# Order of SyncE's transfers in a group, and of two steps of VectorE in the seventh tile

## The reference

```python
q = rope(rms_norm((x @ Wq.T)))                      # 16 heads
k = rope(rms_norm(concat(context, x) @ Wk.T))       # 4 heads, 1857 rows
v = concat(context, x) @ Wv.T
x = x_before + softmax(q @ k.T * SCALE) @ v @ Wo.T
# then: 32 routed experts (6 per token) and a shared one,
# a windowed latent attention over the same context, a small quantised feed-forward
```

## Time and profile before

| | us |
|---|---|
| runs | 1920.83, 1919.81, 1908.78 |
| median | 1919.81 |
| profiled execution | 1917.32 |
| its span, first to last instruction | 1915.5 |
| mean granted clock of TensorE | 0.949 of 2.4 GHz |

### The profile page before, as it was taken

How to read it: one execution, slowest core, us unless ns; L and a number is a source line. 1 busy time by engine, 2 the same in 40 slices (tenths; PEclk the granted TensorE clock), 3 DMA queues, 4 the chain that set the end, 5 groups by cost and what they waited for, 6 DMA issues and landing times. The chain is left out here.

```text
span 1915.5 us, 42600 instructions
## 1 busy us (share of the span) xinstructions
PE 1684.7 (88%) x14901; PEld 1305.6 (68%) x15047; DVE 1422.2 (74%) x3606; ACT 1157.2 (60%) x2910; POOL 1123.2 (59%) x1718
## 2 busy tenths in 40 slices
PE   4899988998999899999898989897899888479987
PEld 3677776787787677777676777675565555339974
DVE  7898886887878788788686868776767565575746
ACT  6577775776777577677665767664325544173533
POOL 5678684786856768568484766741037776182210
PEclk8899999999999999999999999999799999795998
DMA  3210212112020221211113121244639998400100
GB/s 122 73 52 28 68 59 75 52 53 84 24 65 18 76 80 52 68 41 54 53 47 103 52 80 47 68 125 143 219 98 308 304 297 262 179 25 20 45 10 25
DMA packets 117150, 174.91 MB, mean 91 GB/s; under 512 B 13738, under 2 KB 82195, under 8 KB 116691
## 3 DMA queue, kind: packets, MB, share of 16 engines
q1 hardware_dynamic: 106130, 139.99, 22.7%
q0 software_dynamic: 9984, 30.42, 5.2%
q10 hardware_dynamic: 832, 1.84, 0.3%
HBM read 129.04 MB, written 43.16 MB: 90 GB/s over the span
## 5 line engine op out<-in xcount | busy, mean ns | idle before, releaser
L939 DVE TENSOR_TENSOR att_pT<-att_pT 128x512 bf16<-128x512 f32 (+1 forms) x512 | 320.6, 650 | 203.1 <-ACT att_pT L744 200.4
L580 PE MATMUL att_out<-att_V,att_pT 128*128 128x128 bf16 x5760 | 394.9, 221 | 38.3 <-DVE att_pT L939 36.0
L580 PEld LDWEIGHTS att_out<-att_V,att_pT 128*128 128x128 bf16 x5760 | 355.1, 99 | 68.7 <-DVE att_pT L939 53.7
L744 ACT ACTIVATE att_pT<-att_pT 128x512 bf16<-128x512 f32 (+1 forms) x512 | 277.7, 572 | 104.2 <-PE att_pT L566 104.2
L750 ACT ACTIVATE att_prob<-att_scores,att_negmax 128x512 f32<-128x512 f32 (+1 forms) x512 | 329.8, 654 | 17.6 <-DVE att_negmax L928 16.9
L557 PE MATMUL att_scores<-att_K,att_Q 128*128 128x512 bf16 (+1 forms) x1408 | 298.5, 359 | 7.4 <-DVE att_Q L900 0.5
L926 DVE TENSOR_REDUCE att_mx<-att_scores 128x1 f32<-128x512 f32 (+1 forms) x512 | 291.1, 629 | 0.8 <-PE att_scores L557 0.6
L566 PE MATMUL att_pT<-att_ident,att_prob 128*128 128x128 f32 x1920 | 275.7, 275 | 0.0
L557 PEld LDWEIGHTS att_scores<-att_K,att_Q 128*128 128x128 bf16 x1536 | 150.8, 98 | 144.2 <-issue 2.1
L566 PEld LDWEIGHTS att_pT<-att_ident,att_prob 128*128 128x128 f32 x1920 | 210.3, 142 | 1.0
L480 PE MATMUL att_aux<-att_wkv,att_kvT 128*128 128x256 bf16 x1350 | 173.5, 279 | 20.7 <-DVE att_aT L900 16.1
(11 more groups left out here) (352 smaller groups left out, 3302.4 us busy)
## 6 DMA issues: line engine op xcount, KB each, us to landing
moe_wu<-wu_s SPq DMA_DIRECT2D x80, 352.0 KB
att_stage<-in_we_l SPq DMA_DIRECT2D x32, 528.0 KB, 4.7
wu_s<-att_windows SPq DMA_DIRECT2D x32, 352.0 KB, 2.8
moe_wd<-wd_s SPq DMA_DIRECT2D x80, 128.0 KB
att_wq<-wq_s SPq DMA_DIRECT2D x12, 512.0 KB, 4.2
att_wo<-wo_s SPq DMA_DIRECT2D x12, 512.0 KB, 3.8
wd_s<-att_windows SPq DMA_DIRECT2D x32, 176.0 KB, 3.0
att_stage<-in_ctx_l SPq DMA_DIRECT2D x9, 512.0 KB, 4.3
```

The lines of the kernel that those rows point to most:

```text
L580: last = nc.tensor.matmul(out_ps[:, i % 2, :], pT[:, i % 2, a, k, :], V[:, par, k, w, :], start=(k, a, w) == (0, 0, 0), stop=(k, a) == (KT ...
L744: nc.scalar.activation(pT[:, i % 2, 0, 4 * j:4 * j + m, :], pT_ps[j % 2][:, 0:m, :], ACT.Copy).then_inc(s["pt_hi"], 1)
L939: nc.vector.tensor_tensor(pT[:, i % 2, 1, 4 * j:4 * j + m, :], pT_ps[j % 2][:, 0:m, :], pT[:, i % 2, 0, 4 * j:4 * j + m, :], ALU.subtract) ...
```

## The change

In SyncE's program of a group the jobs of this group are listed first (`here`), and those of slot 0 (`early`). Behind L409 come now the stage load for the job after the group's first and the stores of the slot 0 jobs; the near keys' store and the table loads follow; then the remaining jobs. In VectorE's slot the places amid are done before `extra` in slot 6, the places behind after it; other slots have the same order as before.

```diff
--- before.py
+++ after.py
@@ -407,14 +407,23 @@
                     if g >= 3 and g + 1 < groups:
                         sp.wait_ge(s["wo_done"], nth("WO", 1, g - 1))
                         sp.dma_start(wo[:, 1 - par, :, :, :].rearrange("p a h n -> p (a h n)"), t["wo_s"][(g + 1) % KVH]).then_inc(wo_load[1 - par], 16)
+                    here = [j for j, (at, _) in enumerate(JOBS_AT) if at[0] == g]
+                    early = [j for j in here if JOBS_AT[j][0][1] == 0]
+                    if here:
+                        while ahead < len(SPLITS) and ahead <= here[0] + 1:
+                            split_load(ahead)
+                            ahead += 1
+                    for j in early:
+                        split_store(j)
                     if g:
                         near_store(g - 1)
                         near_table(g)
-                    for j in [j for j, (at, _) in enumerate(JOBS_AT) if at[0] == g]:
+                    for j in here:
                         while ahead < len(SPLITS) and ahead <= j + 1:
                             split_load(ahead)
                             ahead += 1
-                        split_store(j)
+                        if j not in early:
+                            split_store(j)
                     if g == 2:
 
                         sp.wait_ge(s["start_stored"], 16 * (1 + len(START_ON_POOL)))
@@ -1042,9 +1051,11 @@
                         probs_low(tile - 1, oi, 3)
                     for kind, n in projected(i, prep):
                         raw_rows(kind, n, g + 1, 1 - u)
+                    for x_ in amid:
+                        task(*x_, g, u)
                     if i == 6 and not last:
                         extra(i, g)
-                    for x_ in amid + behind:
+                    for x_ in behind:
                         task(*x_, g, u)
                     if last:
                         return
```

## The result

The changed kernel takes 1883.64 us in the median of four runs (1882.24 to 1892.14), the kernel before 1917.28 us over four runs; the ratio is 0.9842, with an interval of 0.9803 to 0.9881. By the medians that is 33.6 us less, by the ratio 30.3; I had forecast 23.4, a ratio of 0.9878, which lies just inside the interval. The two profiled executions lie 25.2 us apart (spans 1915.5 and 1890.3): the changed kernel's profile fell on its slowest run.

A forecast was written before the change was run, and what follows sets the result against it. TensorE is busy 88% of the span; eight slot 2 stalls wait on a DMA, and TensorE waits for VectorE's residual sum. 13.2 + 10.2 = 23.4 us off the median 1919.8 gives 1896 us, range 1882 to 1909.

The forecast's parts named there:

- eight stalls of slot 2: Slot 2 of groups 3, 5, 7, 9, 11 to 14: a DMA ends last, making the slot 14.5 to 17.6 us.
- One for one: In the eight stalled slots, whatever brings the last DMA forward was claimed to shorten the span by the same amount.
- The first part: SyncE's near keys' store and tables move behind a load and two expert stores: 1.65 us a stall, 13.2 us in all.
- two readings: Gain per stall by issue time, 1.65 us, or by transfer time of bytes leaving the front, 1.34, 1.95 or 1.2 us.
- upper bound: Slot 2 stalls: the load for slot 6 partly leaves the competition too, giving 2.75 us each, 22 us.
- rival (b): Slot 2: larger stall gain, 2.75 us each, plus up to 1 us each of TensorE clock; 37 us, 1883; chance 0.12.
- The second part: VectorE in slot 6 adds the residual before the job's split, removing TensorE's wait; 10.2 us net, bounds 5 and 16.
- Slot 7: Seven groups give nothing back, 9.5 us kept; of six with an expert, four keep 0.15 us, two lose 0.4 each.
- Rival (a): Waits at slot 7 or the next slots take back all of VectorE's gain in slot 6; 1907 us, chance 0.17.
- (c): Rival: SyncE's later near store and tables get waited for, in slot 3 or GpSimd's rotation; 1948 us, chance 0.04.
- (d): Rival: no effect; something else sets the store's end and slot 7 eats slot 6's gain; 1915 to 1920, chance 0.09.

The follow-up runs named there:

- e3: The changed kernel with the stage load and early stores moved ahead of SyncE's wait for the output projection and the reload of wo; 1852.9 us, ratio 0.9645.
- e5: The changed kernel with the reload of wo moved behind the stage load and early stores, the wait for the projection staying in front; 1867.3 us, one run.
- e1: The changed kernel with VectorE's old order, so SyncE's new order alone; 1902.6 us, ratio 0.9907.
- e4: The changed kernel with GpSimd's rotation of near keys in groups 0, 4 and 8 held until VectorE's angle steps are done; 1892.0 us, one run.
- e2: The kernel before with VectorE's new order in slot 6 alone, SyncE's order old; 1904.9 us, ratio 0.9926.
- e7: e3 with GpSimd's rotation of near keys held until VectorE's extra work of slot 7 is done; 1848.7 us in one run, timed again 1846.1, ratio 0.9625.
- e6: e3 with the fourth expert of groups 3, 7, 11 to 14 and the second of 5 and 9 in slot 4 instead of 7; 1854.6 us, 0.9646.

## Why the prediction was right, and where it was off

**What bounds.** Right in that the eight stalls of slot 2 were a DMA's end: e3 removes them and slot 2 falls by 55.4 us, where the waits had been 54.2. "One for one" is not shown by that; the agreement is luck. Where the clock stays at 1.00, a slot is longer by 1.4 to 2.1 us less than ScalarE's wait: in the seven such groups of e5, 10.3 us for waits of 22.7. (Why is not shown; presumably nobody needs ScalarE for that long.) Before, that made some 14 us less than the waits, and the half clock behind the stalls some 15 more. So a wait that shrinks but stays is worth what it loses, and the clock besides, as in the change and in e5; of one that goes altogether 1.4 to 2.1 us are worth nothing. That is why e3 won 38.0 us by the last 42.9.

**The first part, size.** I took 1.65 us a stall, 13.2 in all. The six store waits fell by 2.16, 1.15, 2.19, 0.59, 1.95 and 1.96, the two context waits by 0.25 and 1.03: 11.3 us, 1.4 a stall. The term that is off is the size of a stall's gain. My two readings do not differ in the sum: issue time makes 8 x 1.65 = 13.2, transfer time 3 x 1.34 + 4 x 1.95 + 1.2 = 13.0. Group by group neither fits: by the bytes groups 5, 9, 13 and 14 should have won most, and 5 and 9 won 0.25 and 1.03 us, while groups 3 and 11 won 2.2, more than either reading gives. The upper bound, that the load of slot 6 leaves the competition, showed no sign in the sum. e1 and e4 have SyncE's new order too, and the eight waits fall by 10.6 and 9.6 us there: groups 3, 7 and 14 by 1.1 to 2.2 in all three kernels, group 12 by 0.6 to 0.9, the context waits by 0.3 to 1.3, groups 11 and 13 by anything from 0.7 to 2.2. That group 12 and the context loads get little thus repeats; why stays open.

**The clock, priced too low and in the wrong place.** Slot 2 fell by 17.3 us with waits that fell by 11.3. The other 6 us are TensorE's clock, which I had put at nothing in the sum, and at most at 1 us a stall, inside rival (b). That 1 us was group 3's slot 2 less group 4's (8.46) less the wait (7.46); but group 3's own slot 2 takes 9.59 us without a stall (e3), and a wait counts for 2 us less than its length. Windows of the kernel before, group 11 (length, busy us of PE, PEld, DVE, ACT, POOL, then granted clock, DMA share, GB/s):

```profile
951.00:955.00 4.00, 1.06 (x3) 0.43 (x4) 0.61 (x1) 2.30 (x6) 0.00 (x0) 0.56 0.11 39
955.00:959.00 4.00, 3.78 (x29) 2.94 (x29) 2.57 (x8) 2.83 (x9) 2.52 (x4) 0.59 0.00 0
```

And of the changed kernel, same group, then group 5:

```profile
935.00:939.00 4.00, 2.08 (x18) 1.26 (x18) 1.29 (x3) 3.32 (x9) 0.53 (x2) 1.00 0.49 162
939.00:943.00 4.00, 4.00 (x37) 3.16 (x36) 2.68 (x8) 3.59 (x11) 3.46 (x6) 1.00 0.21 73
...
470.00:474.00 4.00, 4.00 (x24) 3.31 (x23) 1.17 (x2) 1.58 (x5) 3.92 (x6) 0.50 0.38 133
```

Before, TensorE came out of every one of the eight stalls at 1.2 GHz for a while. After, in groups 9, 11 and 13 it kept 2.4 GHz. There, slot 2's excess over its normal length is 1.4 to 2.1 us less than ScalarE's wait; in groups 3, 7 and 14, with a short stretch at half clock, 0.1 to 0.6 less; in 5 and 12, with a long one, 0.6 to 1.0 more. Against the excess at full clock (group 12 taken like 13 and 14, as no run shows it at full clock) a long stretch (some 6 us at 1.2 GHz) costs 1.9 to 2.8 us and a short one (3 to 4) 0.9 to 1.6: 15.3 us in all before and 9.2 after, which are the 6. Whether it comes depended on more than the wait: group 11 kept its clock with a wait of 5.57 us, group 5 lost it with one of 5.16. That is also what slot 2 won in e2, whose waits had not changed in sum: group 5 kept its clock there, and groups 7 and 11 had a short stretch instead of a long one.

**The second part, slot 6.** Right in its mechanism: TensorE's wait gone, VectorE's idleness from 1.38 to 0.21, 1.4 us in 13 groups and 0.6 in two, 19.6 in all. I had 18.0: by the smaller of the two waits the seven groups with 1.24 or 1.27 on TensorE should have won that, and won 1.4, and groups 6 and 10 won 0.6, not 0.44.

**Slot 7, wrong in two places of opposite sign.** I wrote that in groups 0, 1, 2, 4, 5, 8 and 9 nothing in slot 7 takes anything back, because no store is waited for. Six of the seven gave back 0.53 to 0.90 us, 4.3 together. I had asked what waits for the moved split, and not what now runs beside VectorE's next work: GpSimd (e4, e7). In the six groups with an expert in slot 7 I kept 0.15 us and lost 0.4 in two; the waits of 0.79 grew to 2.27, near the 2.5 predicted, but slot 7 took back only 0.64 to 0.78 of 1.4 us, so 0.7 was kept, and in groups 7 and 14, whose store had been late before, all of it (the 2.44 of the earlier trace rows was 2.19 after). Group 6 shows +0.82 in the changed kernel and 0.01 in e2: the clock again (0.50 for some 3 us there, 1.00 in e2). Slots 6 and 7 together: the seven groups kept 5.5 us of the 9.5, groups 6 and 10 kept 0.4 of the 0.9, and the six groups with an expert kept 6.2 where I had booked a loss of 0.2. Net for the part: 19.6 - 7.5 = 12.1 against 10.2.

**Sum.** First part 11.3 + 6 of clock against 13.2; second part 12.1 against 10.2. Less 0.6 of slot 0 the slots show 28.8 us against 23.4: short by the 6 us of clock, while the errors of the two parts, -1.9 and +1.9, cancel by luck, the second being itself a difference of 4.5 lost and 6.4 won. Rival (b) had the right direction for that: its clock term came, its larger stall did not. That the median, 1883.6, falls on (b)'s 1883 is luck too: (b) needed 37 us, and the slots have 28.8. Rival (a) fell in e2, (c) and (d) with the result.

**The Trainium skill's rate.** The section that I drew on, "Anatomy of one DMA", gives its fit for DMAs that GpSimd issues; these are SyncE's. At 436 GB/s I had some 8 us for the first part; the waits fell by 11.3, and e5's 2.0 us for 512 KB are 262 GB/s. In this stretch of stores, loads and small packets 244 to 269 GB/s came nearer than the page's figure.

## What to carry to other kernels

When a queue's owner stands at a wait, look at what is ordered behind it that has long been ready: moving them to the front behind the wait gave 1.4 us a stall, moving them ahead of the wait gave all of it. Price the bytes in front at the rate that the trace shows for that stretch (2.0 us for 512 KB here), and price TensorE's clock behind the stall with it. See how much of a wait reaches the pace of the kernel: here the last 1.4 to 2.1 us did not. A wait that is removed shifts everything after it: list what the other engines do at that time, and also the engine that nobody waits for; a wait is worth less than its length, and work moved to remove it may cost more where it lands (e6: 22.3 us of waits gone gave 13, the moved splits took 16).

## What the runs showed of the hardware that I had not expected

**VectorE and GpSimd hold each other up, and it is a wait, not a slowing.** VectorE's TENSOR_SCALAR of 128x960 takes 0.65 us alone and 1.07 to 1.12 beside GpSimd's TENSOR_TENSOR; the split of 128x1056 takes 1.25 and 1.79 us; GpSimd's own 0.73 us becomes 1.02 and 1.74. Holding GpSimd back restores all of VectorE's. In the rows above each later instruction ends about its own length after the end of the earlier one. In group 4 GpSimd's L1125 ends at 439.33 and VectorE's L1001 0.51 us later, GpSimd's L1127 0.59 after that, VectorE's L1003 0.52 after that; in group 5 GpSimd's L1127 ends at 521.85 and the split 1.12 later. Each is the time alone less 0.13 or 0.14. The Trainium skill, "SBUF — State Buffer", section "Who interferes with whom", names a pair of ports that the two share: an instruction of VectorE in one of its modes with two ports contends with GpSimd, and so does one with two inputs in SBUF; the one that issues second is blocked until the first is through. The trace agrees for both kinds, within that 0.14 us.

**A DMA's issue can take longer on SyncE.** With two stores of 528 KB in all and the near keys' store issued just ahead of it, the issue of the first table load took 1.63 us instead of 0.50 in group 3, and 1.49 to 1.87 in all the stalled groups but 12. In e3, where the stores leave 10 us earlier, it took 0.49. Why was not tried.
